# The last batch of a transformer tower on one Trainium2 core: maxima of the long tiles and half of a norm placed earlier, router logits taken from centred tokens, one set of transposes placed later

## What is computed

```python
h = concat([cls, tok(x) @ W.T])               # (8, 1 + 1024, 64)
E = layernorm(h); Q, K, V = E@WQ.T, E@WK.T, E@WV.T
S = Q @ K.T / 8
A = exp(S - max(S, -1)) * where(S == 0, 0, tril)
h = h + (A / (sum(A) + 1e-9)) @ V
x = layernorm(h)                               # second norm
w = softmax(mean(x, axis=0) @ Wr + br)         # router: mean over the 8 batches
y = relu(bn2(relu(bn1(x @ W1)) @ W2)) @ Wo + bo      # 8 experts
h = h + sum_over_experts(y * w)
```

## Time and profile before

| what | value |
|---|---|
| median of three runs | 383.86 us |
| the profiled execution | 382.6 us, its span 380.9 us |
| mean granted clock of TensorE in it | 0.963 |
| TensorE busy | 356.5 us, 94% of the span |
| VectorE, ScalarE, GpSimd busy | 71%, 52%, 35% |
| share of TensorE in the chain that ended last | 82% |

### The profile page before, as it was taken

One profiled execution on the slowest core, in us unless ns is written; L12 is line 12 of the kernel. 1 busy time (PEld: TensorE's weight loads), 2 busy tenths in 40 slices (PEclk: granted clock), 3 DMA queues, 4 the chain that ended last, 5 costly groups with the idle time before them and its releaser, 6 DMA issues.

```text
span 380.9 us, 7929 instructions
## 1 busy us (share of the span) xinstructions
PE 356.5 (94%) x2682; PEld 170.9 (45%) x2682; DVE 270.7 (71%) x582; ACT 199.7 (52%) x402; POOL 133.5 (35%) x201
## 2 busy tenths in 40 slices
PE   4889999999999999999999987897999999999985
PEld 2565335356356355355357444352564333333331
DVE  3122867889989989989999989676315566766673
ACT  0224656568468478377387686664535344444410
POOL 7051302525625626626627538315302900000000
PEclk9999999999999999999999999896559999999999
DMA  6999741904605505500000000000000011100112
GB/s 154 224 219 186 147 79 37 186 0 98 128 0 109 113 0 118 102 0 0 2 2 3 0 2 1 2 0 2 1 0 3 2 28 29 29 12 18 29 28 57
DMA packets 28991, 20.44 MB, mean 54 GB/s; under 512 B 12280, under 2 KB 28832, under 8 KB 28960
## 3 DMA queue, kind: packets, MB, share of 16 engines
q1 hardware_dynamic: 28352, 19.91, 25.8%
q10 hardware_dynamic: 608, 0.12, 0.2%
HBM read 17.93 MB, written 2.10 MB: 53 GB/s over the span
## 4 chain that ended last, share of the span: by engine, by line
PE 82%; DVE 5%; issue 4%; ACT 4%; POOL 2%; DMA 1%; SPq 0%; DVEq 0%; POOLq 0%; ACTq 0%
PE Sp L1406 13%; PE Sp L1553 8%; PE MM L1461 6%; PE MM L1687 6%; PE PTB L1418 6%; PE PTB L1665 6%; PE MM L1339 6%; PE MM L1342 5%; PE MM L1469 2%; PE MM L1316 2%; PE Sp L1288 2%; PE MM L1320 2%; PE PTB L1388 1%; POOL st L479 1%; PE Sp L1707 1%
## 5 line engine op out<-in xcount | busy, mean ns | idle before, releaser
L1406 PE MATMUL Sp<-eT,G 64*64 64x512 f32 x512 | 63.7, 599 | 0.2 <-issue 0.2
L449 POOL TENSOR_SCALAR_AFFINE_SELECT EP<-EP 128x128 f32<-128x128 f32 x64 | 23.6, 368 | 103.1 <-ACT EP L654 103.0
L591 ACT ACTIVATE PT<-PTB 128x512 f32<-128x512 f32 (+3 forms) x88 | 38.9, 484 | 26.4 <-PE PTB L1418 23.8
L945 DVE TENSOR_SCALAR_CACHE_REDUCE EP<-Sp,sr 128x1024 f32<-128x1024 f32 x32 | 40.3, 1279 | 5.6 <-PE Sp L1406 5.6
L945 DVE TENSOR_SCALAR_CACHE_REDUCE SN<-Sp,sr 128x1024 f32<-128x1024 f32 x32 | 39.9, 1276 | 1.2 <-PE Sp L1406 1.2
L1406 PEld LDWEIGHTS Sp<-eT,G 64*64 64x64 f32 x512 | 18.8, 133 | 31.4 <-issue 31.2
L1553 PE MATMUL Sp<-E2T,W1f 64*64 64x512 f32 x216 | 31.8, 688 | 0.1
L1461 PE MATMUL MM<-PT,e 128*64 128x512 f32 (+3 forms) x168 | 31.6, 513 | 0.0
L955 DVE SCALAR_TENSOR_TENSOR SN<-SN,EP 128x384 f32<-128x384 f32 (+7 forms) x32 | 27.4, 855 | 4.4 <-ACT EP L657 2.3
L1237 DVE SCALAR_TENSOR_TENSOR EP<-PTB,negc,PTd 128x512 f32<-128x512 f32 x28 | 19.7, 746 | 13.3 <-PE PTB L1665 13.3
L955 DVE SCALAR_TENSOR_TENSOR EP<-EP 128x128 f32<-128x128 f32 (+7 forms) x32 | 27.3, 853 | 2.2 <-ACT EP L657 1.9
(11 more groups left out here) (334 smaller groups left out, 699.3 us busy)
## 6 DMA issues: line engine op xcount, KB each, us to landing
XW<-in_x_dram SPq DMA_DIRECT2D x6, 1024.0 KB, 10.7
X<-in_x_dram SPq DMA_DIRECT2D x6, 1024.0 KB, 9.5
out_dram<-xc SPq DMA_DIRECT2D x8, 256.0 KB, 2.6
XW<-in_x_dram SPq DMA_DIRECT2D x2, 576.0 KB, 7.9
X<-in_x_dram SPq DMA_DIRECT2D x2, 576.0 KB, 14.2
XW<-in_x_dram SPq DMA_DIRECT2D x2, 448.0 KB, 11.2
X<-in_x_dram SPq DMA_DIRECT2D x2, 448.0 KB, 14.2
EP<-in_L_tok_W_dram SPq DMA_DIRECT2D x2, 144.0 KB, 3.3
```

The costliest lines, as they stand in the source:

```text
L449: pool.affine_select(out=blk_, in_=blk_, compare_op=ALU.is_ge, fill=0.0, base=0, pattern=[[-1, 128]], channel_multiplier=1).then_inc(tri_d ...
L591: return act.activation(dst, src, ACT.Copy)
L945: dve.tensor_scalar(W4[p % 4], Sp[p % 2][:, :], -SCALE, sr[q][:, place(t), 0:1], ALU.mult, ALU.min, accum_out=negm[q][:, t:t + 1]).then_in ...
L1406: ins = pe.matmul(Sp[p % 2][64 * s:64 * s + 64, CH * c:CH * c + CH], G[q][rows, 128 * t + 64 * s:128 * t + 64 * s + 64], eT[q][rows, :], **ON)
```

## The change

Names in the order rows: `MM` is the bank pair with halves `M0`, `M1`; `U0` is the buffer for `u_last`; `W1f`, `W2f` are expert weights; `WrB` router weights; an L1553 of before is an L1560 after, L1406 is L1413, L1418 is L1425, L1437 is L1444, L1477 is L1484.

The diff, cut to what the prediction speaks of (the tables of semaphore steps and the class token's moves are left out):

```diff
-        NMID = 5
+        NMID = 4
...
-                add_up(b, 1, pz, 0)
                 tri(b, 6, True)
                 tri(b, 7, True)
-                ln2_rstd(b - 1)
+                add_up(b, 1, pz, 0)
                 class_h()
                 add_up(b, 0, pzl, 1)
+                class_rstd()
+                ln2_rstd(b - 1)
...
             pt_copy(b, 0, True)
+            expo(b, 1, 2, True)
             pt_copy(b, 1, True)
-            expo(b, 1, 2, True)
...
+            expo(b, 1, 6, True)
             h1_wide(3)
-            ln2_sq(b - 1)
+            expo(b, 1, 7, True)
+            act.wait_ge(dve_steps, nth("k_neg", 1))
+            act.activation(clsS[:, 3:4], clsS[:, 2:3], ACT.Exp).then_inc(act_steps, 1)
...
             copy(UT[:, :], M1[:, :]).then_inc(u_done, 1)
             pt_copy(b, 4, True)
-            expo(b, 1, 6, True)
             pt_copy(b, 5, True)
-            expo(b, 1, 7, True)
-            act.wait_ge(dve_steps, nth("k_neg", 1))
-            act.activation(clsS[:, 3:4], clsS[:, 2:3], ACT.Exp).then_inc(act_steps, 1)
             act.wait_ge(p0_arg, 2 * b + 2)
             act.activation(pzl[:, 1, :], pzl[:, 0, :], ACT.Exp).then_inc(p0_exp, 1)
+            pt_copy(b, 6, True)
+            pt_copy(b, 7, True)
             h1_wide(4)
-            pt_copy(b, 6, True)
...
+            ln2_sq(b - 1)
             h1_wide(5)
...
+            h1_wide(6)
+            act.wait_ge(pe_steps, nth("q_x7", 1))
+            copy(XT[:, 2 * 128:CH], M1[:, 2 * 128:CH]).then_inc(act_steps, 1)
+            last_sq("B", slice(0, QG))
+            act.wait_ge(pe_steps, nth("q_x7", 2))
+            copy(XT[:, 0:2 * 128], M1[:, 0:2 * 128]).then_inc(act_steps, 1)
+            e2t_copy(b - 1, M0)
             h1_wide(7)
             h1_wide(8)
-            e2t_copy(b, M1)
             h1_wide(9)
...
+            e2t_copy(NB - 1, Sp[1])
...
+            class_arg(b, 1, 1, 0)
+            smax(b, 1, 6, True)
             o_norm(b - 1, 1)
-            class_arg(b, 1, 1, 0)
             mask(b, 1, 4, True)
-            ln2_centre(b - 1)
+            smax(b, 1, 7, True)
+            class_max()
             mask(b, 1, 5, True)
-            class_max()
-            smax(b, 1, 6, True)
+            class_arg(b, 1, 0, 1, pzl)
+            mask(b, 1, 6, True)
             p0_rest(b, 1, 1, 0)
-            smax(b, 1, 7, True)
-            class_arg(b, 1, 0, 1, pzl)
-            ln2_ss(b - 1)
-            mask(b, 1, 6, True)
             class_weight()
             mask(b, 1, 7, True)
             p0_rest(b, 1, 0, 1, pzl)
             class_centre()
+            ln2_centre(b - 1)
+            class_ss()
...
+            dve.wait_ge(pool_steps, nth("t_rstdB", 1))
             dve.wait_ge(pe_steps, nth("q_lg", 1))
-            dve.wait_ge(dve_steps, nth("q_lga", 1))
-            dve.scalar_tensor_tensor(out=gl9[:, 0:NT, :], in0=M0[:, 0:64].rearrange("p (t e) -> p t e", e=NEXP),
+            dve.tensor_tensor(glx[:, :].rearrange("p (i c e) -> p i c e", i=QG, c=2),
+                              M1[:, 0:64].rearrange("p (c i e) -> p i c e", i=QG, c=2),
+                              st[:, 3, :].rearrange("p (c i) -> p i c", c=2).unsqueeze(3).to_broadcast([128, QG, 2, NEXP]),
+                              ALU.mult).then_inc(dve_steps, 1)
+            dve.wait_ge(dve_steps, nth("q_x", 1))
+            dve.scalar_tensor_tensor(out=gl9[:, 0:NT, :], in0=glx[:, :].rearrange("p (t e) -> p t e", e=NEXP),
                                      scalar=1.0 / NB, in1=gl9[:, 0:NT, :], op0=ALU.mult, op1=ALU.add).then_inc(dve_steps, 1)
-            dve.wait_ge(dve_steps, nth("q_lgb", 1))
+            dve.wait_ge(dve_steps, nth("q_add", 1))
             dve.reduce_max(gs9[:, 0, :], gl9[:, :, :], AX).then_inc(dve_steps, 1)
             dve.wait_ge(dve_steps, nth("q_mx", 1))
             dve.tensor_tensor(gl9[:, :, :], gl9[:, :, :], bc(gs9[:, 0, :], NEXP), ALU.subtract).then_inc(dve_steps, 1)
+            last_e(1, A).then_inc(dve_steps, 1)
+            last_e(0, B).then_inc(e2_done, 1)
...
-                    pe.wait_ge(act_steps, nth("q_bcc", 4))
+                    pe.wait_ge(e2t_done, NB)
...
+            score(b, 1, 6, True)
             pe.wait_ge(r0_done, NB)
             pe.wait_ge(e2t_done, b - 1)
             pe.transpose(M0[0:8, 0:128], r0min[:, :], ident[:, :]).then_inc(pe_steps, 1)
             o_group(b - 1, 1)
+            score(b, 1, 7, True)
             layer1(3, NCH * b + 8)
-            score(b, 1, 6, True)
-            score(b, 1, 7, True)
...
-            layer1(4, NCH * b + 10)
-            pe.wait_ge(h1_done, 10)
+            pe.wait_ge(negm_done, 8 * NB - 1)
+            layer1(4)
             p_turn(b, 6, paired=True, down=True)
-            pe.wait_ge(negm_done, 8 * NB)
-            layer1(5)
+            p_turn(b, 7, paired=True, down=True)
             pe.wait_ge(pt_done, NCH * b + 11)
             pe.wait_ge(dve_steps, nth("k_max", 1))
             u_last(QG, M0, 128)
-            p_turn(b, 7, paired=True, down=True)
             pe.wait_ge(pt_done, NCH * NB)
-            u_last(1, Sp[0], 0)
+            u_last(1, PTp[0], 0)
+            pe.wait_ge(negm_done, 8 * NB)
+            layer1(5)
...
+            def x_turn(x, bank, first, last):
+                for i in range(first, last):
+                    ins = pe.transpose(bank[:, 128 * i:128 * i + 128], x[:, 2 * i:2 * i + 2, :], ident[:, :])
...
+            pe.wait_ge(dve_steps, nth("t_hA", QG))
+            x_turn(xc, M1, 2, QG)
...
+            pe.wait_ge(dve_steps, nth("t_centB", 1))
+            pe.wait_ge(act_steps, nth("q_x7c", 1))
+            x_turn(xc, M1, 0, 2)
+            e2_turn(b - 1, M0)
             layer1(8)
             pe.wait_ge(facc_done, NB)
             for i in range(QG):
-                pe.matmul(M0[:, 16 * i:16 * i + 16], facc[:, 0, 128 * i:128 * i + 128], WrB[:, :], **ON)
-            pe.matmul(M0[:, 64:72], f64[:, :], WrB[0:64, 0:NEXP], **ON).then_inc(pe_steps, 1)
-            e2_turn(b, M1, e2=e32[0])
+                pe.matmul(PTp[0][:, 16 * i:16 * i + 16], facc[:, 0, 128 * i:128 * i + 128], WrB[:, :], **ON)
+            pe.matmul(PTp[0][:, 64:72], f64[:, :], WrB[0:64, 0:NEXP], **ON).then_inc(pe_steps, 1)
+            pe.wait_ge(act_steps, nth("q_x7c", 2))
+            for i in range(QG):
+                ins = pe.matmul(M1[:, 16 * i:16 * i + 16], XT[:, 128 * i:128 * i + 128], WrB[:, :], **ON)
+            ins.then_inc(pe_steps, 1)
             layer1(9)
-            pe.wait_ge(e2t_done, NB)
+            pe.wait_ge(pool_steps, nth("bn_w2", 1))
             pe.wait_ge(dve_steps, nth("q_lga", 1))
-            for i in range(QG):
-                ins = pe.matmul(M0[:, 16 * i:16 * i + 16], E2T[:, b, 128 * i:128 * i + 128], WrB[:, :], **ON)
...
             layer3(0, 1)
+            def last_turn():
+                pe.wait_ge(act_steps, nth("q_bcc", 4))
+                pe.wait_ge(e2_done, NB)
+                for i in range(QG):
+                    ins = pe.transpose(L1p[1][0][:, 128 * i:128 * i + 128], e32[0][:, 2 * i:2 * i + 2, :], ident[:, :])
+                ins.then_inc(e2t_ready, 1)
             for b in range(1, NB):
                 layer2(b, 0)
                 layer3(b - 1, 2)
+                if b == 1:
+                    last_turn()
                 layer3(b - 1, 3)
                 layer2(b, 1)
                 for n in L1_AT[b][0]:
```

57 lines of the change are left out of this document (24 added, 33 removed).

## The result

The changed kernel takes **372.38 us** (median of four runs: 371.1, 371.37, 373.38, 374.36) against 384.13 us for the kernel before in the same measurement: a ratio of 0.9703, 95% interval 0.9647 to 0.9758. The forecast was 375.6 us, range 371 to 380. The profiled execution took 371.37 us, its span 369.6 us; the kernel before had 382.6 and 380.9.

What follows compares the result with a forecast made beforehand. TensorE was taken to bound, at half clock from 260.6 to 284.5 us. Terms: 2.25 - 1.3 - 0.76 + 11.5 = 11.7, less 3.4 for a new fall, 8.3 us saved: 375.6 us, range 371 to 380.

Steps and rivals of the forecast that it cites:

- a fall behind two waits: At 260.6 us the clock falls to 0.50 until 284.5, following TensorE waits of 0.51 and 1.37 us.
- Part 1: Around the short transposes, waits of 0.51, 1.37 and 0.37 us go: 2.25 us gone, 1.3 us of new waits.
- new waits: At `u_last` 0.55 us and at the sum over batches 0.75 us, together taken as 1.3 us lost.
- Part 2: Four new transposes of centred tokens (0.66 us) and four moved to the expert stage (0.1 us): 0.76 us added.
- Part 3: TensorE's 22.97 us of busy time in the low stretch take half at full clock: 11.5 us saved.
- The sum without a fall: If the clock never falls in this stretch: 2.25 - 1.3 - 0.76 + 11.5 = 11.7 us saved.
- The likeliest case: Behind the router's row of small products, a fall at about 270 to 272 lasting 6.8 us; 375.6 us, 42%.
- rival (1): No fall at all behind the router's small products: 372.2 us, chance 25%.
- The term of 3.4 us: Cost of the expected 6.8 us fall behind the router's small products, taking 11.7 us saved to 8.3.
- (3): Fall at 260.6 stays and ends as before; only waits count, about 0.9 us saved, 383.0 us, chance 8%.
- (4): Low clock of (3) carries on through the stage that spreads the gates, to 298: 389.7 us, chance 5%.
- The rule that was weighed: Skill page: without a long idle gap TensorE keeps full clock; by that 11.7 us saved, 372.2 us.

Runs made afterwards that it cites:

- e1: The kernel before, in its own order, with four dense fill products put into its two waits of 0.51 and 1.37 us; 382.60 us.
- e8: The kernel before with e1's four fill products and four more in the waits of 1.07 and 0.92 us, nothing moved; 373.98 us.
- e5: The changed kernel with the router as before, reading normed tokens, without the transposes of centred tokens; 370.41 us.
- e2: The changed kernel with NMID 5 again, so the transposes of p = 6 wait for the wide activation's bank; 374.02 us.
- e3: The changed kernel with the two scores of p = 6 and 7 behind layer1(3) again on TensorE; 373.24 us.
- e4: The changed kernel with five dense fill products in TensorE's first idle time of 2.65 us; 369.93 us.
- e6: The changed kernel with layer1(9) moved up between the router's small products; 370.90 us.
- e11: e4 with the router's eight products of 16 columns each issued twice; 374.09 us.
- e12: e4 with two dense fill products of 240 columns in the 0.40 us wait ahead of the router's first product; 370.45 us.

## Why the prediction was right, and where not

- **The clock bounds, and a fall behind two waits is what the change removes**: right, and shown by e1, in which the fall at 260.6 goes with the two waits filled, and by e8, which holds the full clock without moving a step. The clock stays at 1.00 from 243.5 to 360 us in the profiled execution.
- **Part 1, waits gone**: right. The wait for `h1_wide` is gone, the maximum of p = 6 ends at 251.97 (forecast "about 251.7"). The new waits were put too high: 0.36 us ahead of `u_last` where 0.55 was taken, 0.40 at the sum over batches where 0.75 was. Together 0.76 instead of 1.3 us. A wait of 0.17 us for an `h1_wide`, at 274.47 behind the router's products, was not foreseen.
- **Part 2, added and moved**: forecast 0.76 us, measured 0.96 by e5. The cover for the copies held.
- **Part 3, 11.5 us for the clock**: the sum holds, but how it splits depends on what is taken first, and the text did not see that. Taken first, in the old order, the full clock is worth only 7.9 to 9.0 us (e8), because waits of 1.07 and 0.92 us come to light that the earlier trace rows do not have, and fills don't make them shorter. The change removes these two as well: in it TensorE has no idle time at `layer1(6)` or at the class token's transpose, since class and residual work stand earlier on VectorE (a reading of the order, which no run tests by itself). The order is then worth 2.3 to 3.4 us, where the prediction's terms (2.25 - 1.3 - 0.76) gave 0.2. The 11.5 us themselves were not measured, as no run has the new order at the low clock; that the total came out all the same is in part luck, since nothing in the text makes the two hidden waits go. The fault is a method: half of the busy time at the low clock is an upper bound for what the full clock returns, until the other engines' work in that stretch is laid beside the shorter time. The text did that by sums of busy time (9.8 us in 12), which says nothing of a chain.
- **The sum without a fall**: 11.7 forecast, 380.9 - 369.6 = 11.3 measured.
- **The likeliest case, one short fall at 270 to 272**: this is the step that failed for the number. The profiled execution has none; it is rival (1), whose 372.2 us is within 0.2 of the median measured. That closeness is partly luck, as this median lies between two runs at 0.995 (371.1 and 371.37) and two with more low clock (373.38 and 374.36). The mechanism exists (e2, e3, e4, e6, e11 and e12 each show a fall between 269.6 and 279.1), but e4's runs, from 368.0 at 1.00 to the profiled 372.41 with the fall, show it as one outcome of a program and not, as the text put it, the sure consequence of the order. The term of 3.4 us for it was mis-sized, too: five of those six falls lasted 3.4 us, half of the 6.8 taken, and e4's, the only one of 6.8, cost 2.9 us.
- **Rivals (3) and (4)**, the fall at 260.6 staying: no profile of the changed kernel or its variants shows it, not even e2 with its 1.38 us wait back. The 0.9 us saved in (3) don't follow from its own terms: four new transposes at the low clock are 1.11 us, so it is 2.25 - 1.3 - 1.11 + 0.45 = 0.3, and the time 383.6 instead of 383.0.
- **Two readings of rows.** The dense run in which the first fall ended is of 128x512 products (240.08, L1461), not 64x512. And not "every product" takes twice its time at the low clock: four transposes take 1.11 against 0.66 us, which is 1.7 times. Neither changes the sum.
- **The rule that was weighed**: by the Trainium skill (TensorE: Matmul & The Clock Gate, the part on HAM oscillation) a kernel without a long idle gap keeps its clock. The traces agree at the first fall, behind 2.65 us of idle time, which e4's fill removes. It does not hold for the late one, which in e12 came at 270.7 with the wait ahead of it filled.

## What to carry to other kernels

Read the granted clock beside the busy time: a stretch that is 100% busy at 1.2 GHz is the first thing to mend, and dense products that compute nothing, put into the waits ahead of it, show what the clock is worth and which waits it was hiding (e1, e8). Fill every wait of the group, not the first pair only, or the fall moves to the next (e1). Before moving work to shorten such a stretch, leave out one part of the change at a time: here the part with the most code, the router from centred tokens, cost 0.96 us and gave nothing back that a run shows.
